# A fused state-space and attention kernel: the first chunk's first MLP moved from the last unit of the scan to right behind the scan

## The reference

```python
# block 0: two selective state-space passes (forward and backward in time), then an MLP
h, gate = adaln(x, c, mamba_w, mamba_b)            # layernorm, then scale and shift from c
x = x + gate * (ssm(h, fwd) + flip(ssm(flip(h), bwd)))
h, gate = adaln(x, c, mlp_w, mlp_b)
x = x + gate * ((silu(h @ mlp_w1) * (h @ mlp_w2)) @ mlp_w3)      # hidden size 512
# ssm, per token t, 512 inner channels x 64 states:
#   hst = hst * exp(dt_t * A) + (dt_t * x_t) * B_t ;  y_t = sum over states of hst * C_t
# block 1: attention with 16 heads of 16, then an MLP with hidden size 1024
x = x + attention(adaln_rms(x, c), mask)
x = x + mlp(adaln_rms(x, c))
```

## Time and profile before

| what | us |
|---|---|
| median of 3 runs | 3348.09 |
| lowest and highest run | 3346.66, 3351.29 |
| the profiled execution, its own time | 3350.24 |
| its span, first to last instruction | 3348.5 |
| TensorE busy, whole span | 3222.0 (96%) |
| VectorE busy | 2912.5 (87%) |
| ScalarE busy | 2833.3 (85%) |
| POOL busy | 2314.1 (69%) |

### The profile page before, as it was taken

One profiled execution on the slowest core, in us unless ns is written; L12 is line 12 of the kernel. 1 busy time (PEld: TensorE's weight loads), 2 busy tenths in 40 slices (PEclk: granted clock), 3 DMA queues, 4 the chain that ended last, 5 costly groups with the idle time before them and its releaser, 6 DMA issues.

```text
span 3348.5 us, 59371 instructions
## 1 busy us (share of the span) xinstructions
PE 3222.0 (96%) x22634; PEld 2519.8 (75%) x22634; DVE 2912.5 (87%) x2859; ACT 2833.3 (85%) x4648; POOL 2314.1 (69%) x1105
## 2 busy tenths in 40 slices
PE   8999999999999999999999999999899978999899
PEld 5888898999999999999999899999787432222244
DVE  4999999999999999999999999999997587888131
ACT  6999999999999999999999999999896325777620
POOL 1789999999999999999999999999776000000000
PEclk9999999999999999999999999999999988999999
DMA  3222222222222222222222222222111044321000
GB/s 116 69 78 77 84 70 73 66 70 72 71 90 72 72 72 72 72 72 72 75 69 74 70 70 69 72 70 90 56 56 51 0 101 96 46 37 31 13 7 19
DMA packets 199901, 218.82 MB, mean 65 GB/s; under 512 B 80033, under 2 KB 149665, under 8 KB 199361
## 3 DMA queue, kind: packets, MB, share of 16 engines
q1 hardware_dynamic: 199618, 215.02, 22.7%
HBM read 194.29 MB, written 18.19 MB: 63 GB/s over the span
## 4 chain that ended last, share of the span: by engine, by line
PE 73%; ACT 17%; DVE 6%; issue 3%; DMA 1%; SPq 0%; POOL 0%; DVEq 0%; ACTq 0%
PE psum L1594 20%; PE psum L1362 17%; PE psum L1588 15%; PE psum L1585 11%; ACT arena L1045 7%; ACT arena L1027 6%; PE psum L1672 3%; PE psum L1661 3%; PE psum L1645 2%; DVE arena L1272 2%; DVE row_max L1315 2%; PE psum L1614 1%; ACT arena L1069 1%; ACT L1051 0%; DVE arena L1127 0%
## 5 line engine op out<-in xcount | busy, mean ns | idle before, releaser
L1272 DVE TENSOR_TENSOR_SCAN arena<-arena,psum 128x512 f32<-128x512 f32 x2048 | 2373.5, 1228 | 66.8 <-PE psum L1588 52.8
L770 POOL TENSOR_TENSOR arena<-arena 128x1024 f32<-128x1024 f32 x1024 | 2221.5, 2181 | 282.1 <-DVE arena L1272 258.4
L1045 ACT ACTIVATE arena<-arena,a_neg 128x512 f32<-128x512 f32 x2048 | 1445.5, 727 | 38.8 <-PE psum L1588 38.0
L1594 PE MATMUL psum<-ident,arena 128*128 128x128 f32 x8192 | 1234.0, 274 | 1.6 <-POOL arena L770 1.6
L1027 ACT ACTIVATE arena<-arena,bT 128x512 f32<-128x512 f32 x1536 | 1115.0, 726 | 0.0
L1588 PE MATMUL psum<-ident,arena 128*128 128x128 f32 x6144 | 1011.8, 274 | 0.0
L1594 PEld LDWEIGHTS psum<-ident,arena 128*128 128x128 f32 x8192 | 964.8, 142 | 2.1 <-POOL arena L770 2.1
L1585 PE MATMUL psum<-arena 128*128 128x128 f32 x4096 | 822.7, 283 | 39.8 <-DVE arena L1272 21.6
L1585 PEld LDWEIGHTS psum<-arena 128*128 128x128 f32 x4096 | 649.7, 192 | 254.0 <-issue 151.7
L1588 PEld LDWEIGHTS psum<-ident,arena 128*128 128x128 f32 x6144 | 746.1, 142 | 0.0
L1362 PE MATMUL psum<-arena 128*128 128x512 f32 (+1 forms) x1440 | 680.6, 594 | 19.5 <-DVE arena L1147 8.0
(11 more groups left out here) (114 smaller groups left out, 945.0 us busy)
## 6 DMA issues: line engine op xcount, KB each, us to landing
arena<-bc_dram SPq DMA_DIRECT2D x256, 512.0 KB, 3.7
arena<-diag_dram SPq DMA_DIRECT2D x224, 128.0 KB, 2.1
arena<-qk_dram SPq DMA_DIRECT2D x96, 128.0 KB
diag_dram<-arena SPq DMA_DIRECT2D x32, 256.0 KB, 4.4
qk_dram<-arena SPq DMA_DIRECT2D x12, 512.0 KB, 4.9
arena<-in_x SPq DMA_DIRECT2D x4, 512.0 KB, 10.1
arena<-skip_w SPq DMA_DIRECT2D x64, 32.0 KB, 2.0
arena<-sums_dram SPq DMA_DIRECT2D x64, 32.0 KB, 1.8
```

Source lines behind the costliest of these rows:

```text
L770: pool.tensor_tensor(out[:, :, way], h_now[:, :, way], c_row, ALU.mult)\
L1045: act.activation(decay[:, w % AHEAD, f], dt_[:, u % 2, f], ACT.Exp, scale=a_neg[:, d, f, st:st + 1])\
L1272: dve.tensor_tensor_scan(hs[:, w % RING, f, rows][:, way], decay[:, w % AHEAD, f, way], psum[:, 4 + n % U_BANKS, way], end_state(w - DS, f ...
L1594: return pe.matmul(psum[:, c, f * P:(f + 1) * P], hs[:, w % RING, f, at:at + P], ident[:, :], is_transpose=True, start=False, stop=w % DS ...
```

## The change

The eight up tiles and the two down tiles of the MLP of chunk 0 (in the order of "ln1") leave the list of unit 7's turns and stand at the head of LATE, ahead of yT and out of unit 7. N0 is 8, so they are the same ten tiles, and every tile keeps its number; the banks of the ten are now 4 to 7 in turn. The `act_turns` of steps 36 and later no longer contain "up" entries, so neither the silus nor the table loads that go with them stand there.

```diff
@@ turns(u), the list for unit 7 @@
             yT_ = [("yT", u - 1, f) for f in range(NI)]
             zs_ = [("zs", u, c) for c in range(TB)]
             out_ = [("out", u - 1, c) for c in range(C)]
-            return yT_ + zs_ + out_ + steps("mean", "ln1", 0, 1, 2) + steps("sum", "ln1", 0, 1, 2)\
-                + up("ln1", 0, 0, 8) + [("down", "ln1", 0, c) for c in range(C)]
+            return yT_ + zs_ + out_ + steps("mean", "ln1", 0, 1, 2) + steps("sum", "ln1", 0, 1, 2)
...
-        LATE = [("yT", UNITS - 1, f) for f in range(NI)] + [("out", UNITS - 1, c) for c in range(C)] + steps("mean centre square", "ln1", 3)\
+        LATE = up("ln1", 0, 0, N0) + down("ln1", 0) + [("yT", UNITS - 1, f) for f in range(NI)] + [("out", UNITS - 1, c) for c in range(C)] + steps("mean centre square", "ln1", 3)\
             + up("ln1", 1, 0, N0) + down("ln1", 1) + up("ln1", 2, 0, 4) + steps("sum std recip scale", "ln1", 3) + steps("square", "rms0", 0, 1)\
```

## The result

| | us |
|---|---|
| before, median of 20 runs | 3349.31 (3345.86 to 3353.32) |
| changed, median of 20 runs | 3354.32 (3351.52 to 3357.91) |
| ratio, 95% interval | 1.0015 (1.0008 to 1.0022) |
| profiled execution of the changed kernel, span | 3355.0 (before 3348.5) |

The change costs 5.0 us, 0.15%: slower, but within the 0.2% that the prediction called no change. Forecast were +6.6 us and a range of 3350.5 to 3359.5.

The account below looks back on a forecast made before the run. VectorE was taken to bound unit 7's scan and TensorE the stretch behind it. The scan saves 3.8 + 4.1 + 1.8 = 9.7 us, TensorE adds 16.3: +6.6 on 3348.09 gives 3354.7 us, range 3350.5 to 3359.5.

Parts of the forecast that it names:

- In unit 7 VectorE's work and gaps are counted: Unit 7 of the scan: only VectorE's work and gaps count; ScalarE costs time only where VectorE shows idle time.
- ScalarE needs 4.3 us of its 4.69: Unit 7: ScalarE issues seven instructions a step, 4.3 us, while VectorE's four scans take 4.69 us.
- VectorE's own work: Unit 7: four gates at 0.61 us and two updates at 0.66 us leave VectorE, saving 3.8 us.
- The waits late in the unit: Late in unit 7: VectorE's gaps of 1.49 and 2.37 us from late silus go, saving 4.1 us with overlaps.
- The waits behind the reciprocals: Unit 7, after the two last reciprocals: VectorE's gaps of 0.81 and 0.97 us go, saving 1.8 us (bounds 0 and 1.8).
- TensorE behind the scan: Last transposes to the last chunk's mean: 32.6 us in place of 16.3, adding 16.3 us.
- The clock holds: TensorE behind the scan: up tiles fill the third wait, so full clock stays; 0 us added, against 3.4 if it falls.
- The rival that ScalarE bounds the scan: Unit 7: ScalarE's silus and lone reloads, 17.9 us, all shorten the scan; sum -1.6 us, 3346.5; chance 0.06.
- A later stretch at the lower clock: Rival, TensorE around 2644 to 2648 us: the shift spares a low-clock stretch, 3.4 us; sum +3.2, 3351.3; chance 0.12.

Follow-up runs that it names:

- copy_for_silu: Kernel before, with a plain copy for the first chunk's four silus and without the table loads around them: 3347.24 us, ratio 0.9993.
- down_only: Kernel before, with only the two down tiles moved to the head of LATE and the eight up tiles left in unit 7: 3349.36 us, ratio 0.9996.
- ups_three_later: Kernel before, with the up and down tiles of unit 7's turns three steps later (39 to 62): 3350.79 us, ratio 1.0001.
- behind_out: Changed kernel, with the ten tiles behind yT and out instead of ahead of them: 3360.88 us, ratio 1.0030 to the kernel before.
- no_lone_reload: Kernel before, without the four table loads that follow the odd up tiles, where no silu stands: 3347.74 us, ratio 0.9992.
- next_ups_first: Kernel before, with the next chunk's eight up tiles, already in LATE, put at its head: 3345.35 us, ratio 0.9984.
- next_ups_no_lone: Kernel before, with the edits of next_ups_first and no_lone_reload together: 3341.39 us, ratio 0.9975.
- all_three: Kernel before, with the edits of next_ups_first, no_lone_reload and ups_three_later together: 3337.39 us, ratio 0.9964.

## Why the prediction was right, point by point

- **Sign and size.** +6.6 forecast, +5.0 measured, interval +2.7 to +7.4. The chance went slightly more to "slower by over 0.2%" (0.56) than to "within" (0.41); the median fell within. With the forecast set on the bound that was close to a coin. Of the 1.6 us by which the forecast was too high the traces account for 1.4: the scan gave back 10.9 us instead of 9.7, and TensorE behind it cost 16.1 instead of 16.3.
- **In unit 7 VectorE's work and gaps are counted.** Right as a count; copy_for_silu and the 108 scans at 1.173 us show it. But what the count stands for is narrower than "VectorE decides": between the second and the fourth silu ScalarE set the pace with its rounds of 21.94 us (the chain of waits names it there in turn with TensorE), and VectorE's gaps are the part of the difference that showed. The prediction's "ScalarE needs 4.3 us of its 4.69" holds for a step without a silu; with one silu and one empty load in four steps it needs 5.5.
- **VectorE's own work, 3.8 us.** Right as far as it was tried: down_only alone gives 1.4 us for the two updates, against 1.3 by the step. The gates can be read with them: copy_for_silu's stretch (141.48) is 5.75 us longer than the changed kernel's (135.73), and the 3.8 us of this term with the gaps of 0.64 and 0.97 us behind the third reciprocal (1.83 with the overlaps) make 5.6.
- **The waits late in the unit, 4.1 us.** Right: 4.3 us in copy_for_silu, and none left in the changed kernel.
- **The waits behind the reciprocals, 1.8 us.** Undersized. The step took only the two gaps that an up matmul fills; the 0.64 us gap between them went too. 0.81 + 0.64 + 0.97 and 0.11 us of overlap for each make 2.75 us, and with that the scan's sum is 10.7 us against 10.9 in the ledger. Before, the clock was at 0.50 from 2436 to 2440; in the changed kernel it was at 0.81 and in ups_three_later at 0.76, both without the gap. That this is the cause was not tried.
- **TensorE behind the scan, +16.3 us.** Right: +16.1. By piece, forecast and then measured: up tiles and gate 14.7 and 14.7 (2562.73 to 2577.41), down tiles 6.9 and 7.0, yT to out 3.0 and 2.8, out to mean 8.0 and 7.95.
- **The clock holds.** Right. It fell in each of the five traces in which the wait for the gating stayed open (before, behind_out, copy_for_silu, no_lone_reload, ups_three_later), and held in the five in which matmuls fill it (the changed kernel, down_only, next_ups_first, next_ups_no_lone, all_three). The reason given, that it fell only once the third wait had begun, holds in all five, but the margin was small: read in windows of 0.2 us the fall comes 0.5 us (ups_three_later) to 3.6 us (before) behind the end of the last transposes. The prediction knew only the 3.6.
- **The rival that ScalarE bounds the scan.** It fell with copy_for_silu: 15 us less of ScalarE's work gave 4.3 us in the trace. By the Trainium skill, page "ScalarE: Activation LUTs", section "What ACT_TABLE_LOAD costs", each switch of tables would carry a drain of about 1.38 us as well; no run here shows one, the next instruction starts 0.02 us behind the load.
- **A later stretch at the lower clock.** It did get shorter, by 1.1 us in the profiled execution. One execution of each can't say whether that is so in the median; the 1.6 us by which the forecast was too high are nearly used up by the two terms above.

## What to carry to other kernels

An engine's pauses are worth filling, but fill them with work that this engine has to do later anyway: moving work from a stage where it is a guest to a stage that the engine bounds pays for every record beyond the pause. Count what another engine costs in the gaps of the engine that otherwise runs without pause, not in its own time and not in the chain of waits, which can change engine without any change of the pace. To say what a relief will bring, set the round of the one (four steps with a silu, 21.94 us) against the round of the other (19.35 us): relief beyond the difference brings nothing. Before moving a step, ask what hid it where it stood: the silu beside the reciprocal was free, and three steps later there was one slow round more.

## What the runs showed of the hardware

Waits of 0.41, 1.24 and 2.58 us, with two bursts of 1.1 us between them, were enough for the granted clock to go from 2.4 to 1.2 GHz (1.00 to 0.50), and the next 32 records took 3.0 to 3.9 us longer for it: yT 2.71 us (before) or 3.67 us (copy_for_silu) against 1.91, out 9.30 or 9.27 us against 7.11. Filling the last of the three waits alone, with 7, 14 or 21 us of matmuls, avoided it each time, although in one trace (ups_three_later) the fall came when that wait was only 0.5 us old.

An activation table load took 1.28 us in all these rows, also where the wanted table had just been loaded and nothing had used another since (2468.87).
